# One sort key read into a register ahead of the first transfers instead of two, and all eight read at once after them

## The chip, the cores and the metric

The kernel runs on one core of a Trainium2 chip. The metric is the device time of one execution in microseconds (us); lower is better. In the profile the engines are called PE (TensorE, the matrix engine; PEld is its weight load), DVE (VectorE), ACT (ScalarE), POOL (GpSimd) and SP (SyncE, which here only issues transfers). A name with a q behind it (SPq, PEldq, POOLq) is an engine's own instruction queue: register loads, waits and DMA issues.

## The reference

```python
def _L0_cond_ref(x, cat_ids, W, b):
    selected_W = W[cat_ids]
    selected_b = b[cat_ids]
    return jnp.einsum('bti,bio->bto', x, selected_W) + selected_b[:, None, :]
x = x + _L0_cond_ref(x, itok_B_0_30, L0_cond_W, L0_cond_b)
```

x is [128, 128, 512] in float32: 128 batches of 128 rows. Each batch has a class, drawn from 0 to 30; W holds 32 matrices of 512x512 and b 32 rows of 512. Each batch is multiplied by its class's matrix, the class's bias row is added, and x itself is added.

## The kernel before, in words

The batches are worked in the order of their class, so that each class's weights are loaded once. In this data class 0 has six batches, class 1 three and class 2 nine, out of 128 batches in all. The residual is folded into the weights: GpSimd adds 1 to their diagonal (L236, L244, L260). float32 precision is reached with three products of rounded parts: xh and wh are the high parts of x and W, xl and wl the rests, and a batch is 12 matmuls (four slices of the contraction, three products), all at L436 except for the first batch. A chunk of 128 of the 512 contraction rows of a class's weights is called a chunk here; the weights of class 0 come as chunks 0 and 1 together (L284), chunk 2 (L285) and chunk 3 (L173), those of class 1 as two halves (L163).

The order of the batches is found on the chip. The ids arrive (L160), VectorE makes one sort key for each batch out of id and position (L328) and takes the eight largest (`top`, L330); the batch numbers of the first eight batches in sorted order follow from these keys. The full order, `tbc`, follows later (L343). SP needs a batch's number in a register before it can issue the load of its x, since the number is part of the address: `load(i)` takes it from `first[i]` (L168) for the first eight batches and from `tbc` afterwards (L150, eight at a time).

SP issues in the order of its program: x of batch 0, chunk 3 of class 0's weights, x of batch 1, first half of class 1's weights, then x of batches 2 and 3, bias row 0, the second half of class 1's weights, x of batch 4, the weights of class 2 (after a wait for the first batch's matmuls, L195 and L196), x of batch 5, bias row 1, and on with one x load and one store a batch.

```python
eng.wait_ge(s_t0, 1)
eng.load(first[:2], top[0:1, 0:2])
```

Each x goes through ACT (xh at L299, a copy into PSUM at L302) and DVE (xl at L348). The first batch is special: its first two slices are multiplied unsplit as soon as x has landed (L450), the other two in parts (L460), for which chunk 3 passes POOL (L236), ACT (L306) and DVE (L357). Class 1 is split by POOL in two halves (L244, L246, L248), every later class whole (L260, L268, L272). The bias rows of classes 2 and 3 are loaded by POOL behind the weights of class 3, which POOL issues once class 1 is split and bias row 1 has landed (L251). PE may begin class 2 only when these bias rows have landed (L277, then the semaphore `s_w`). Batches 6, 7 and 8 are of class 1; batch 9 is the first of class 2.

Of the kernel before, what the change touches and what calls it, by code (L numbers as in the profile page):

```python
# [5 lines left out]
def cond_resid(nc, xt, ids, W, bias, out):  # L6
# [31 lines left out]
    with ExitStack() as ctx:  # L38
        def sb(name, shape, dt):
            return ctx.enter_context(nc.sbuf_tensor(name, shape, dt))  # L40
# [25 lines left out]
        top = sb("top", [1, 8], i32)  # L66
# [57 lines left out]
        def raw(c, k0, k1):  # L124
            return wr[:, c % NR, k0 * D:k1 * D]
# [11 lines left out]
        def bias_load(eng, j0, j1, done):  # L137
            at = slice(j0 * D, j1 * D)
            eng.dma_start(bb[:, at].rearrange("p (c d) -> p c d", c=j1 - j0),  # L139
                          bias[j0:j1, :].rearrange("(a c) d -> a c d", a=1).to_broadcast([128, j1 - j0, D]))\  # L140
               .then_inc(done, 16)

        def table(eng, name, src, n, lo, hi, ahead=8):

            regs = [eng.alloc_register(f"{name}{i}") for i in range(ahead)]

            def get(i):
                if i % ahead == 0:
                    m = min(ahead, n - i)
                    eng.load(regs[:m], src[0:1, i:i + m])  # L150
                return eng.snap(regs[i % ahead], min_val=lo, max_val=hi)
            return get

        def x_load(eng, i, b):
            eng.dma_start(xs[:, i % NX, :, :], xt[b, :, :].rearrange("a p (k t) -> (a p) k t", k=KT))\  # L155
               .then_inc(s_x[i % NX], 16)

        @block.sync
        def _(eng):
            eng.dma_start(idr[:, :], ids.rearrange("(a n) -> a n", a=1)).then_inc(s_id, 16)  # L160
            def w1_load(h):
                k0, k1 = W1[h]
                eng.dma_start(raw(1, k0, k1), W[1, :, k0 * D:k1 * D]).then_inc(s_w1[h], 16)  # L163

            first = [eng.alloc_register(f"first{i}") for i in range(8)]

            def sorted_first(i):
                return (B - 1) - eng.snap(first[i], min_val=0, max_val=C * B - 1) % B  # L168

            eng.wait_ge(s_t0, 1)  # L170
            eng.load(first[:2], top[0:1, 0:2])  # L171
            x_load(eng, 0, bass.ds(sorted_first(0), 1))
            eng.dma_start(raw(0, 3, KT), W[0, :, 3 * D:]).then_inc(s_w0[2], 16)  # L173
            ahead = table(eng, "la", tbc, B, 0, B - 1)
            behind = table(eng, "st", tbc, B, 0, B - 1)

            def load(i):
                b = sorted_first(i) if i < 8 else ahead(i)
                if i == NX:
                    eng.wait_ge(s_xb, 2)  # L180
                    eng.wait_ge(s_mm, 2)
                elif i > NX:
                    eng.wait_ge(s_pt, i - NX)
                x_load(eng, i, bass.ds(b, 1))

            load(1)
            w1_load(0)
            eng.load(first[2:], top[0:1, 2:])
            load(2)
            load(3)  # L190
            bias_load(eng, 0, 1, s_b0[0])
            w1_load(1)
            load(4)
            eng.wait_ge(s_wd, KT)
            eng.wait_ge(s_raw, 1)  # L195
            eng.dma_start(wr[:, 0, :], W[2, :, :]).then_inc(s_w2, 16)  # L196
            load(5)
            bias_load(eng, 1, 2, s_b0[1])
            eng.wait_ge(s_tab, 1)
            for i in range(B):  # L200
                if i + AHEAD < B:
                    load(i + AHEAD)
                b = behind(i)
                eng.dma_start(out[bass.ds(b, 1), :, :].rearrange("a t d -> (a t) d"), os[:, i % NO, :])\
                   ._wait_ge(s_fin, i + 1).then_inc(s_o[i % NO], 16)
            for i in range(B - NO, B):
                eng.wait_ge(s_o[i % NO], 16 * (i // NO + 1))
# [285 lines left out]
```

## Time and profile before

| | before |
|---|---|
| median of 3 runs | 361.57 us (361.54 to 361.67) |
| the profiled execution | 361.55 us |
| its span, first to last instruction | 359.8 us |
| granted TensorE clock, mean | 0.999 |
| PE busy | 353.9 us (98%) |
| POOL busy | 268.6 us (75%) |
| DVE busy | 172.9 us (48%) |
| ACT busy | 146.6 us (41%) |
| mean DMA rate | 304 GB/s |

The profiled execution is 0.02 us below the median, and the span leaves out 1.75 us of it, which lie before the first and behind the last instruction. PE is busy almost all the time; the other engines have room on the whole, though not at each moment.

### The profile page before, as it was taken

To read this page: it belongs to the slowest core of one execution; us is meant where nothing else is said; L and a number is where in the kernel's file an instruction comes from. 1 tells how busy PE (TensorE), PEld (TensorE's weight loads), DVE (VectorE), ACT (ScalarE), POOL (GpSimd) and SP (SyncE) were. 2 spreads that over 40 slices of the span, in tenths; PEclk is the share of its full clock that TensorE was granted. 3 is DMA by queue.
4 is the path that set the end of the run, shared out by engine and by line. 5 is a ranking of instruction groups with operands and counts; after the bars stand their busy time and mean duration, and the time that the engine had idled before them with its cause. 6 is when DMAs were issued, how large, how long until landed. Compare 5 with 4: busy or idle time off the path is not lost.

```text
span 359.8 us, 6800 instructions
## 1 busy us (share of the span) xinstructions
PE 353.9 (98%) x1554; PEld 289.4 (80%) x1554; DVE 172.9 (48%) x278; ACT 146.6 (41%) x262; POOL 268.6 (75%) x148
## 2 busy tenths in 40 slices
PE   7999999999999999999999999999999999999996
PEld 2788888888888888888888888888888888888884
DVE  5754454535544454454454454445445445445442
ACT  4554353416443434343343344344344343434420
POOL 3797999998648698799964999799979899934000
PEclk9999999999999999999999999999999999999999
DMA  6999998999986999889996899989997999965532
GB/s 218 334 375 374 383 371 289 305 373 380 310 298 241 366 289 307 301 297 382 352 335 232 289 387 307 341 296 376 318 339 262 369 370 311 316 201 195 183 117 89
DMA packets 43381, 109.51 MB, mean 304 GB/s; under 512 B 4817, under 2 KB 4818, under 8 KB 38610
## 3 DMA queue, kind: packets, MB, share of 16 engines
q1 hardware_dynamic: 37730, 70.01, 54.1%
q0 software_dynamic: 5328, 38.28, 30.9%
q10 hardware_dynamic: 288, 0.79, 0.6%
q8 instruction: 18, 0.29, 0.3%
q14 instruction: 17, 0.14, 0.1%
HBM read 75.50 MB, written 33.55 MB: 303 GB/s over the span
## 4 chain that ended last, share of the span: by engine, by line
PE 96%; DMA 1%; DVE 0%; SPq 0%; issue 0%; ACT 0%; POOL 0%
PE pA L436 96%; DMA wr<-w 1%; DMA idr<-ids 0%; PE pA L460 0%; DVE os L383 0%; SPq L171 0%; ACT wh L306 0%; POOL wr L236 0%; SPq L155 0%; DVE top L330 0%; DVE key L328 0%; SPq L168 0%; PE pA L464 0%
## 5 line engine op out<-in xcount | busy, mean ns | idle before, releaser
L383 DVE TENSOR_TENSOR os<-pA,bb 128x512 f32<-128x512 f32 x128 | 88.5, 691 | 167.0 <-PE pA L436 166.8
L299 ACT ACTIVATE xh<-xs 128x512 fp32r<-128x512 f32 x127 | 80.3, 632 | 195.1 <-PE pA L436 115.7
L272 POOL TENSOR_TENSOR wl<-wr,wh 128x2048 fp32r<-128x2048 f32 x30 | 138.7, 4623 | 2.5
L436 PE MATMUL pA<-wh,xh 128*128 x508 | 135.9, 389 | 0.3 <-issue 0.3
L436 PE MATMUL pA<-wl,xh 128*128 x508 | 135.8, 389 | 0.0
L436 PE MATMUL pA<-wh,xl 128*128 x508 | 135.6, 389 | 0.0
L436 PEld LDWEIGHTS pA<-wh,xh 128*128 128x128 f32 x508 | 95.3, 188 | 20.0 <-issue 0.3
L436 PEld LDWEIGHTS pA<-wh,xl 128*128 128x128 f32 x508 | 95.3, 188 | 19.8
L436 PEld LDWEIGHTS pA<-wl,xh 128*128 128x128 f32 x508 | 95.3, 188 | 19.8
L348 DVE TENSOR_TENSOR xl<-pT,xh 128x512 fp32r<-128x512 f32 x127 | 86.7, 682 | 13.2 <-ACT pT L302 13.1
L268 POOL TENSOR_SCALAR wh<-wr 128x2048 fp32r<-128x2048 f32 x30 | 57.6, 1920 | 36.6 <-PE pA L436 34.8
L302 ACT ACTIVATE pT<-xs 128x512 f32<-128x512 f32 x127 | 74.0, 583 | 0.0
L260 POOL TENSOR_TENSOR wr<-wr,ident 128x512 f32<-128x512 f32 x30 | 39.2, 1305 | 0.7
L226 POOL DMA_DIRECT2D wr<-w x29 | 17.2, 592 | 11.1 <-POOL wl L272 8.0
L236 POOL TENSOR_TENSOR wr<-wr,ident 128x128 f32<-128x128 f32 x4 | 1.8, 472 | 4.5 <-DVE num L340 2.8
L390 PE MATMUL pA<-fill 128*128 128x512 bf16 (+2 forms) x14 | 4.0, 436 | 1.2 <-DVE fill L322 1.2
L248 POOL TENSOR_TENSOR wl<-wr,wh 128x1024 fp32r<-128x1024 f32 x2 | 4.8, 2404 | 0.2
L139 POOL DMA_DIRECT2D bb<-bias x8 | 4.3, 534 | 0.2 <-issue 0.2
L306 ACT ACTIVATE wh<-wr 128x512 fp32r<-128x512 f32 x4 | 2.4, 621 | 3.5 <-POOL wr L236 3.5
L357 DVE TENSOR_TENSOR wl<-wr,wh 128x512 fp32r<-128x512 f32 x4 | 2.7, 691 | 1.7 <-ACT wh L306 1.6
L244 POOL TENSOR_TENSOR wr<-wr,ident 128x256 f32<-128x256 f32 x2 | 1.5, 732 | 2.7 <-DVE wl L357 2.1
L390 PEld LDWEIGHTS pA<-fill 128*128 128x128 bf16 x14 | 1.3, 122 | 2.3 <-issue 2.1
(51 smaller groups left out, 20.1 us busy)
## 6 DMA issues: line engine op xcount, KB each, us to landing
xs<-xt SPq DMA_DIRECT2D x128, 256.0 KB, 5.7
out<-os SPq DMA_DIRECT2D x128, 256.0 KB, 5.1
wr<-w POOLq DMA_DIRECT2D x29, 1024.0 KB, 7.6
bb<-bias POOLq DMA_DIRECT2D x7, 1024.0 KB, 9.0
wr<-w SPq DMA_DIRECT2D x2, 512.0 KB, 5.8
wr<-w SPq DMA_DIRECT2D x1, 1024.0 KB, 8.1
wr<-w ACTq DMA_DIRECT2D x1, 512.0 KB, 3.7
bb<-bias SPq DMA_DIRECT2D x2, 256.0 KB, 6.7
```

The source lines that it names most:

```text
L139: eng.dma_start(bb[:, at].rearrange("p (c d) -> p c d", c=j1 - j0), bias[j0:j1, :].rearrange("(a c) d -> a c d", a=1).to_broadcast([128, j ...
L226: eng.dma_start(wr[:, c % NR, :], W[c, :, :]).then_inc(s_wr[c % NR], 16)
L248: eng.tensor_tensor(wl[:, at], half, wh[:, at].bitcast(f32), ALU.subtract).then_inc(s_wp, 1)
L260: eng.tensor_tensor(eye, eye, ones_on(KT), ALU.add).then_inc(s_ri, 1)
L268: eng.tensor_scalar(wh[:, at], wr[:, c % NR, :], 1.0, 1.0, ALU.mult, ALU.mult).then_inc(s_wh, 1)
L272: eng.tensor_tensor(wl[:, at], wr[:, c % NR, :], wh[:, at].bitcast(f32), ALU.subtract).then_inc(s_wp if c == 2 else s_w, 1)
L299: eng.activation(xh[:, i % NH, :, :], xs[:, i % NX, :, :], ACT.Copy).then_inc(s_xh, 1)
L302: eng.activation(pT[i % NT][:, :, :], xs[:, i % NX, :, :], ACT.Copy).then_inc(s_pt, 1)
L348: eng.tensor_tensor(xl[:, i % NH, :, :], pT[i % NT][:, :, :], xh[:, i % NH, :, :].bitcast(f32), ALU.subtract).then_inc(s_xl, 1)
L383: eng.tensor_tensor(os[:, i % NO, :], pA[i % NA][:, :], bb[:, bass.ds(at, D)], ALU.add)._wait_ge(s_mm, i + 2).then_inc(s_fin, 1)
L390: eng.matmul(pA[0][:, 0:w], fill[:, 0:128], fill[:, 0:w], start=True, stop=True)
L436: mm = eng.matmul(pA[i % NA][:, :], xp[:, i % NH, k, :], wp[:, bass.ds(at + k * D, D)], start=(n == 0), stop=(n == 3 * KT - 1))
```

## The change

SP loads one sort key ahead of batch 0's x and chunk 3, and all eight keys in one load right behind them. The load of the remaining six keys, which stood behind the first half of class 1's weights, is gone.

```diff
             eng.wait_ge(s_t0, 1)
-            eng.load(first[:2], top[0:1, 0:2])
+            eng.load(first[0], top[0:1, 0:1])
             x_load(eng, 0, bass.ds(sorted_first(0), 1))
             eng.dma_start(raw(0, 3, KT), W[0, :, 3 * D:]).then_inc(s_w0[2], 16)
+            eng.load(first, top[0:1, :])
             ahead = table(eng, "la", tbc, B, 0, B - 1)
             behind = table(eng, "st", tbc, B, 0, B - 1)
...
             load(1)
             w1_load(0)
-            eng.load(first[2:], top[0:1, 2:])
             load(2)
             load(3)
```

On SP, at the start of the program, the order changes as follows. TENSOR_LOAD is the load of keys into registers, the two ISA rows in front of a DMA are the arithmetic on its address, `xs<-xt` is an x load, and `wr<-w` a load of weights (128x512 is chunk 3, 128x1024 the first half of class 1).

```order
 L155 DMA xs<-xt 128x512
 L173 DMA wr<-w 128x512
+L174 TENSOR_LOAD top
 L168 ISA
 L155 ISA
 L155 DMA xs<-xt 128x512
 L163 DMA wr<-w 128x1024
-L188 TENSOR_LOAD top
 L168 ISA
 L155 ISA
```

The second load of keys has moved up past two transfers, batch 1's x and the first half of class 1's weights. The number of instructions on SP stays 562, and the orders of the other four engines are the same in both programs.

## Rows read from the trace of the kernel before

**Rows 1.** Waits of PE between 11 and 356 us: total us, times, longest.
```profile
PE pA L436 <- issue: 0.3, 1, 0.3
```

**Rows 2.** Chain that ended last, in order of time: start us, us, what.
```profile
2.66 0.66 SPq L171
...
3.72 0.39 SPq L155
...
4.16 3.81 DMA wr<-w
...
8.03 0.54 POOL wr L236
...
8.59 0.64 ACT wh L306
...
10.78 345.75 PE pA L436 x1524
```

**Rows 3.** Loads into registers by line: min/median/max ns, first and last start us.
```profile
L171 SPq TENSOR_LOAD <-top x1: 663/663/663, 2.7 to 2.7; - x1
...
L188 SPq TENSOR_LOAD <-top x1: 1281/1281/1281, 5.8 to 5.8; - x1
...
L405 PEldq TENSOR_LOAD <-top x1: 487/487/487, 3.2 to 3.2; - x1
...
L150 PEldq TENSOR_LOAD <-tbc x32: 328/332/747, 10.0 to 341.4; - x32
L150 SPq TENSOR_LOAD <-tbc x31: 520/532/1289, 13.1 to 336.5; - x31
```

**Rows 4.** Timeline of SP: start us, us, engine, line, operation.
```profile
4.97 0.34 SPq L155 DMA_DIRECT2D xs<-xt  x1
5.35 0.42 SPq L163 DMA_DIRECT2D wr<-w  x1
...
11.71 0.67 SPq L139 DMA_DIRECT2D bb<-bias  x1
```

**Rows 5.** Transfers issued at 3.72, 4.97, 5.35, 11.71, 21.45: KB, us to landing.
```profile
xs<-xt SPq DMA_DIRECT2D x1, 256.0 KB, 2.7
...
xs<-xt SPq DMA_DIRECT2D x1, 256.0 KB, 3.6
...
wr<-w SPq DMA_DIRECT2D x1, 512.0 KB, 5.1
...
bb<-bias SPq DMA_DIRECT2D x1, 256.0 KB, 8.3
...
bb<-bias POOLq DMA_DIRECT2D x1, 512.0 KB, 10.4
```

**Rows 6.** Busy time by stretch; the last two numbers are DMA share and GB/s.
```profile
6.00:7.00 1.00, 0.57 (x2) 0.34 (x3) 0.69 (x1) 1.00 (x4) 0.34 (x1) 1.00 0.61 172
```

**Rows 7.** Timeline of ACT, PE, POOL: start us, us, operation [idle before <-releaser].
```profile
9.13 0.61 ACT L299 ACTIVATE xh<-xs 128x512 fp32r<-128x512 f32 x1
...
9.27 0.50 PE L460 MATMUL pA<-wh,xh 128*128 128x512 f32 x1 [0.40 <-ACT wh L306]
...
10.63 0.74 POOL L244 TENSOR_TENSOR wr<-wr,ident 128x256 f32<-128x256 f32 x1 [2.07 <-DVE wl L357]
...
15.65 0.73 POOL L244 TENSOR_TENSOR wr<-wr,ident 128x256 f32<-128x256 f32 x1 [0.60 <-DMA wr<-w]
...
20.71 0.74 POOL L226 DMA_DIRECT2D wr<-w  x1 [0.70 <-DMA bb<-bias]
21.45 0.56 POOL L139 DMA_DIRECT2D bb<-bias  x1
```

**Rows 8.** PE's queue, released for batches 1 and 9, then batch 9's first weight load.
```profile
L436 PEldq FUSED_REGOPS  x1: 108/108/108, 10.6 to 10.6; - x1
...
L436 PEldq FUSED_REGOPS  x1: 91/91/91, 31.9 to 31.9; - x1
...
32.44 0.87 PEld L436 LDWEIGHTS pA<-wh,xl 128*128 128x128 f32 x4
```

## The prediction

> **What bounds the kernel now.** I read the waits of PE first. Between 11 and 356 us PE waits for others once, 0.3 us [rows 1]; the chain that ended last says the same, since from 10.78 us on it is 345.75 us of L436 without a break, then the last addition [rows 2]. So there are only two ways for an edit at the start to move the end: the moment at which the unbroken stretch begins, or a hole torn into it. Neither SP nor the transfers bound the middle.
>
> Before 10.78 us the chain is one path [rows 2]: SP reads its keys (2.66 us, 0.66 us long), issues x of batch 0 (3.72) and chunk 3 (4.16); chunk 3 takes 3.81 us to land; then POOL's diagonal (0.54), ACT's high part (0.64) and, from 9.27 on [rows 7], the last four matmuls of the first batch; then batch 1 begins. Chunk 3, not x, is the late one: x landed 2.7 us after its issue [rows 5], at 6.4, chunk 3 at 7.97.
>
> **The change part by part.**
>
> *The first load reads one key and not two.* Everything on the path from 2.66 on moves with it, one for one. The load of two keys took 0.663 us [rows 3]. One key on SP is nowhere in the trace. The nearest row is PE's load of one key from the same tile, half a microsecond later: 0.487. The loads of four registers on PE have a median of 0.332, so a load can be as short as 0.33 at least there; from above, nothing says that one key must be shorter than two. Bounds 0 and -0.33; I take -0.15, close to 0.663 - 0.487 = 0.18 and to the slope of the two loads of `top` on SP, (1.281 - 0.663) / 4 = 0.155 a key.
>
> *Eight keys are read behind chunk 3, and the six-key load is gone.* The new load stands ahead of x of batch 1 and of the first half of class 1. Its length: the SP loads of eight registers from `tbc` have 0.520 / 0.532 / 1.289 (minimum, median, maximum of 31), while six registers from `top`, also right behind two DMA issues, took 1.281 [rows 3]. So the number of registers doesn't set the length alone. The straight line through the loads of `top` gives 0.663 + 6 x 0.155 = 1.59. Bounds 0.52 and 1.59; I take 1.3, the row in the same place of the queue.
>
> The Trainium skill speaks to this in two places. DMA: Bandwidth & Descriptors, Latency and other measured facts, gives a load of this kind a floor of about 600 ns; the rows of 328 and 520 ns lie below it, so here the measurement decides. Runtime: NRT & Kernel Launch, Instruction fetch mechanics, prices such loads at some 200 ns a register; by that rule the first load would save 0.2 and the eight keys would take 1.6, an estimate, while the row of eight registers in 0.532 contradicts it and those of `top` agree roughly.
>
> With 1.3 the issue of batch 1's x goes from 4.97 to 4.97 - 0.15 + 1.3 + 0.04 (the step between two instructions) = 6.16, and class 1's first half from 5.35 to 6.54: both 1.2 us later (0.4 to 1.5 with the bounds). From x of batch 2 on, SP has one load less behind it: removed 1.28, added 1.3, minus 0.15, so about 0.1 earlier (bounds -0.9 and +0.3). Its queue is behind that the same until the wait at L195 for the first batch's matmuls, and bias row 1, issued at 11.71 [rows 4], moves with PE's start.
>
> *Who waits for batch 1's x.* It was issued at 4.97 and took 3.6 us [rows 5], so it landed at 8.6, but ACT came to it at 9.13, from chunk 3's high part, and was done at 9.74 [rows 7]. PE's queue was released for batch 1 at 10.6 [rows 8]. With PE 0.15 earlier, xh must be done by about 10.45, so the landing may be as late as 10.45 - 0.61 - 0.1 = 9.7. Issued at 6.16 it lands at 9.8 with the old 3.6, and at 8.9 with the 2.7 us that batch 0's x took on an otherwise emptier queue. Between 6 and 7 us the DMA engines were busy only 61% of the time at 172 GB/s [rows 6], so the queue isn't full there and the shorter time is the nearer one. Price: 0, with bounds 0 and (issue 6.5, landing 10.1) +0.4.
>
> *Who waits for class 1's first half.* It landed at 10.45 (5.35 + 5.1); POOL took it at 10.63, released by DVE. At 15.65 POOL began the second half, after a wait of 0.60 for its landing, so a half takes 15.05 - 10.63 = 4.4 us [rows 7]. So the first half may be up to 0.6 + 0.2 later for nothing. 1.2 later it costs POOL 0.4, if the transfer keeps its 5.1 us; 1.5 later, 0.7. It went behind batch 1's x in the same queue, and chunk 3 is out of its way now, so I expect 4.5 rather than 5.1, and no delay.
>
> *And class 2.* This is the narrow place behind the start. POOL split class 1 until 20.0 and bias row 1 landed at 11.71 + 8.3 = 20.0 too; then POOL issued at 20.71 and 21.45 the weights of class 3 and the bias rows 2 and 3, which landed 10.4 us later [rows 4, 5, 7], at 31.85. PE's queue went on at 31.9, and the first weight load of batch 9 was at 32.44 [rows 8]. From release to weight load takes about 0.17, as at batch 1 (10.78, the first matmul there, less 10.6); so the spare time there is 0.54 - 0.17 = 0.37 us. A PE that comes 0.15 earlier uses 0.15 of it. No hole, price 0. Later classes have not let PE wait before either [rows 1], and nothing of theirs changes but this shift.
>
> *Chunk 3's own transfer.* It took 3.8 us where x took 2.7, and batch 1's x was issued 0.8 us behind it. If that traffic slowed it, it now lands up to 1.1 earlier. PE could use 0.4 of that, the time for which it stood idle ahead of the matmuls on chunk 3 at 9.27 [rows 7]. The later transfer can hardly slow an earlier one in the same queue, so I take 0 and keep -0.4 as a bound.
>
> **Sum.** -0.15 (first load) + 0 (batch 1's x) + 0 (class 1, class 2) + 0 (chunk 3) = -0.15. Against the profiled execution's 361.55 that is 361.40, and against the median of 361.57 it is 361.42; I say 361.4.
>
> **The rivals.**
>
> *Nothing moves.* One key takes SP as long as two. For it: loads of one, four and eight registers differ less by number than by moment. 361.57.
>
> *Batch 1's x becomes late.* It keeps 3.6 us, the eight keys take 1.3 to 1.6, and PE begins batch 1 up to 0.4 later than it could: 361.4 + 0.1 to 0.4, 361.5 to 361.8. For it speaks that three transfers are in flight; against it the 61% of the DMA share.
>
> *The bias rows of class 2 come late: slower.* Class 1's first half lands 1.2 to 1.5 later, POOL is 0.4 to 0.7 late at 20.71, and the bias rows land that much later. Of this 0.37 is spare, so a hole of up to 0.35: 361.6 to 361.9. The landing of 10.4 us lies in a stretch with full DMA engines; if the new order there makes it 1.1 us later or more (0.37 + 0.72), the kernel ends above 362.3, measurably slower.
>
> *Chunk 3 lands early.* -0.15 - 0.4 = -0.55, and with a first load of 0.33 us -0.73: 361.0 to 360.8. For it speaks the 3.8 us beside the 2.7. But the spare 0.37 at batch 9 stands against it: PE would reach class 2 before its bias rows unless they come earlier too, and the gain ends at 361.2. Only with both is it measurably faster.
>
> **How the numbers follow.** A measurement of this kernel tells a change from none at about 0.2%, 0.72 us: above 362.3 or below 360.85. My forecast has 0.45; nothing moves 0.15; x of batch 1 late 0.13; bias rows late within 0.72 us 0.12, beyond it 0.07; chunk 3 early 0.08, of which 0.04 beyond 0.72. The range reaches from 360.95 (early chunk, not held at batch 9) to 362.1 (a hole of 0.5, bias rows 0.9 late) and leaves out about 0.12. The same cases give faster 0.04, same 0.89, slower 0.07.
>
> **What the profile after would show.** The load at L171 at about 0.5 us; x of batch 0 issued at 3.57 and chunk 3 at 4.0; a load at L174 of about 1.3 us; x of batch 1 issued near 6.2 and landed by 9.7; the unbroken stretch of L436 beginning at 10.6; POOL's second half still begun near 15.6; PE's queue released for batch 9 near 31.9 with no idle time of PE behind 11 us. The prediction is wrong if PE waits for ACT at batch 1, if POOL issues class 3 later than 21.1, or if chunk 3 takes less than 3 us.

## The result, and the profile after

The changed kernel has a median of 360.81 us over 22 executions against 361.68 us of the kernel before over 22, a ratio of 0.9979 with a 95% interval of 0.9972 to 0.9985: faster by about 0.2%, some 0.8 us. The forecast was 361.4, with a range from 360.95 to 362.1, so the result lies 0.14 us below the range.

The median hides how the times lie. Of the 22 executions 16 took 360.71 to 361.02 us, five 361.50 to 361.55, one 362.15. The kernel before never went below 361.51 in 22, and spread from there to 362.51. The profiled execution of the changed kernel is one of its later group: 361.55 us, span 359.8, the same as the profile of before. So the two profiles show what the change did to each step, and the reason why nothing came of it in that execution. The chain that ended last, start and us (to compare with [rows 2]):

```profile
2.67 0.47 SPq L171
...
3.53 0.39 SPq L155
...
3.97 3.81 DMA wr<-w
...
7.85 0.73 POOL wr L236
...
8.60 0.64 ACT wh L306
...
9.29 1.22 PE pA L460 x4
...
10.78 345.73 PE pA L436 x1524
```

The first load is 0.19 us shorter, x of batch 0 and chunk 3 are issued 0.19 earlier, and chunk 3 lands 0.19 earlier. Then GpSimd's fourth addition (L236) begins at 7.85 instead of 8.03 and ends at 8.57 or 8.58 as before: the whole gain is lost in this one operation, which takes 0.73 instead of 0.54 [rows 2]. Its timeline beside VectorE's:

```profile
7.56 0.69 DVE L357 TENSOR_TENSOR wl<-wr,wh 128x512 fp32r<-128x512 f32 x1
7.85 0.72 POOL L236 TENSOR_TENSOR wr<-wr,ident 128x128 f32<-128x128 f32 x1 [1.51 <-DMA wr<-w]
```

The addition begins inside VectorE's operation and ends 0.33 after its end at 8.25. The profile counts four of these additions, of which the median took 0.456 (min/median/max in ns):

```profile
L236 POOL TENSOR_TENSOR wr<-wr,ident x4: 455/456/721, 5.1 to 7.8; 128x128 f32<-128x128 f32 x4
```

The loads of keys, and SP's timeline behind them (against [rows 3, 4]):

```profile
L171 SPq TENSOR_LOAD <-top x1: 470/470/470, 2.7 to 2.7; - x1
...
L174 SPq TENSOR_LOAD <-top x1: 551/551/551, 4.4 to 4.4; - x1
```

```profile
5.35 0.34 SPq L155 DMA_DIRECT2D xs<-xt  x1
5.73 0.43 SPq L163 DMA_DIRECT2D wr<-w  x1
6.54 0.34 SPq L155 DMA_DIRECT2D xs<-xt  x1
```

Eight keys took 0.551 us, not 1.3. Batch 1's x is only 0.38 later than before, and batch 2's x, formerly issued at 7.45, is 0.91 earlier. That reaches far: bias row 1 took 7.5 us instead of 8.3, and the bias rows of classes 2 and 3, issued by POOL 0.02 later than before, landed after 9.2 us instead of 10.4 [rows 5]:

```profile
bb<-bias POOLq DMA_DIRECT2D x1, 512.0 KB, 9.2
```

### The profile page after: what moved, and what is told of

Its sections match the earlier page's. It is cut to its first block, busy times and chain, and to the rows that moved or that the text cites. A ratio compares the mean times of both kernels' runs of the same rounds, so it can differ in the third digit from the quotient of the medians.

```text
span 359.8 us, 6800 instructions
## 1 busy us (share of the span) xinstructions
PE 354.4 (99%) x1554; PEld 289.5 (80%) x1554; DVE 172.3 (48%) x278; ACT 146.6 (41%) x262; POOL 268.6 (75%) x148
## 4 chain that ended last, share of the span: by engine, by line
PE 96%; DMA 1%; DVE 0%; SPq 0%; issue 0%; POOL 0%; ACT 0%
PE pA L436 96%; DMA wr<-w 1%; DMA idr<-ids 0%; PE pA L460 0%; POOL wr L236 0%; DVE os L383 0%; ACT wh L306 0%; SPq L155 0%; SPq L171 0%; DVE top L330 0%; DVE key L328 0%; SPq L168 0%; PE pA L464 0%
## 5 line engine op out<-in xcount | busy, mean ns | idle before, releaser
L436 PE MATMUL pA<-wh,xh 128*128 x508 | 135.9, 389 | 0.3 <-issue 0.3
L436 PE MATMUL pA<-wl,xh 128*128 x508 | 135.8, 389 | 0.0
L436 PE MATMUL pA<-wh,xl 128*128 x508 | 135.6, 389 | 0.0
L436 PEld LDWEIGHTS pA<-wh,xh 128*128 128x128 f32 x508 | 95.3, 188 | 20.1 <-issue 0.3
L436 PEld LDWEIGHTS pA<-wh,xl 128*128 128x128 f32 x508 | 95.3, 188 | 19.8
L436 PEld LDWEIGHTS pA<-wl,xh 128*128 128x128 f32 x508 | 95.3, 188 | 19.8
L236 POOL TENSOR_TENSOR wr<-wr,ident 128x128 f32<-128x128 f32 x4 | 2.0, 522 | 4.3 <-DVE num L340 2.8
L357 DVE TENSOR_TENSOR wl<-wr,wh 128x512 fp32r<-128x512 f32 x4 | 2.7, 690 | 1.4 <-ACT wh L306 1.4
```

Of the source, the lines that this page charges most:

```text
L436: mm = eng.matmul(pA[i % NA][:, :], xp[:, i % NH, k, :], wp[:, bass.ds(at + k * D, D)], start=(n == 0), stop=(n == 3 * KT - 1))
```

## The experiments

In each of the five series the kernel before was timed on the same chip. Its medians were 361.94, 361.94, 361.80, 361.74 and 361.76 us; the lowest of all its 166 executions, those of the result included, is 361.51. An execution below 361.3 us is called early in what follows. Two executions far outside (513.98 us of before, 2053.52 us of one variant) are left out of what follows. "Half" is the first half of class 1's weights.

### First series: is the gain made at chunk 3?

**e1_after_again**: the changed kernel, not edited.

> The changed kernel once more, unchanged, for a profile of an execution near 360.75 us. Theory A (chunk 3 races against a VectorE operation): the times fall into two groups, near 360.75 and near 361.52. In the profile of after, GpSimd's fourth addition (L236) began at 7.85 us, inside VectorE's operation of 7.56 to 8.25, took 0.72 instead of 0.45 us and ended at 8.58, as in the kernel before. In an execution of the faster group chunk 3 should land before 7.3 us, the addition should take about 0.45 and end before 7.9, and L436 should begin near 10.0 instead of 10.78. Theory B (the gain is made at batch 9 or later): L436 begins near 10.78 in both groups, and the difference stands behind it.

Measured: 361.04 us median, 360.74 to 361.56, seven of 11 below 361.3; ratio 0.9977 (0.9968 to 0.9986). The profile fell into the later group again, but is worth more than one of the earlier would have been. Chunk 3 landed 0.27 us sooner than in the other profile, and nothing came of that either:

```profile
7.55 0.69 DVE L357 TENSOR_TENSOR wl<-wr,wh 128x512 fp32r<-128x512 f32 x1
7.58 0.99 POOL L236 TENSOR_TENSOR wr<-wr,ident 128x128 f32<-128x128 f32 x1 [1.24 <-DMA wr<-w]
```

The addition began 0.03 behind VectorE's operation and took 0.99 us, to end at 8.57 once more.

**e2_two_then_eight**: the second part of the change alone.

```diff
-            eng.load(first[0], top[0:1, 0:1])
+            eng.load(first[:2], top[0:1, 0:2])
```

> The changed kernel with two keys, not one, in the first load; eight keys behind chunk 3 as in after. It takes away the 0.19 us that the first load gave and keeps the later issue of batch 1's x. Theory A1 (chunk 3 is faster because batch 1's x and class 1's half come later behind it): a group near 360.8 to 360.95 us remains, median below 361.2. Theory A2 (the 0.19 us of the first load alone carry chunk 3 over the edge): all executions near 361.5, as before.

Measured: 361.54 us median, 360.83 to 362.47; five of 12 at 360.83 to 361.20; ratio 0.9986 (0.9976 to 0.9996). Chunk 3 is issued at 4.16 here as in before, and still there are executions that before never has. So A1 holds in part: what follows chunk 3 matters. With the shorter first load the share is larger (7 of 11 in the same series). Its profile is of the earlier group, 360.94 us. Chunk 3 took 3.3 us, and the addition just went ahead of VectorE's operation:

```profile
7.50 0.46 POOL L236 TENSOR_TENSOR wr<-wr,ident 128x128 f32<-128x128 f32 x1 [1.17 <-DMA wr<-w]
7.55 2.40 DVE L357 TENSOR_TENSOR wl<-wr,wh 128x512 fp32r<-128x512 f32 x3
```

0.08 us decides between this profile and the last: an addition begun at 7.50 ends at 7.96, one begun at 7.58 at 8.57. L436 began at 10.17 instead of 10.78, and there was no idle time of PE behind it.

**e3_vector_waits**: VectorE's second L357 waits until all four additions are done.

```diff
+            eng.wait_ge(s_ri, KT)
             for k in LOW[1:]:
                 low_w(k)
```

> The changed kernel, but VectorE starts its second L357 operation only when GpSimd's fourth addition is done. Theory A (while VectorE's operation on two SBUF inputs runs, GpSimd's addition stands still): the addition takes 0.45 us instead of 0.72 where chunk 3 lands near 7.8; ACT's fourth L306 begins near 8.3, L436 near 10.5, so the slower group moves from 361.52 to about 361.25; the faster group stays. Rival (the addition took 0.72 for a reason of its own, or waits for late bytes of chunk 3): the addition still ends at 8.58 and VectorE only comes later, 361.5 to 361.8.

Measured: 360.98 us median, 360.78 to 361.48; ratio 0.9975 (0.9966 to 0.9984). The times now fill the space: 360.78 to 360.98 (six), 361.13, 361.26, 361.45 to 361.48 (three). None stands at 361.5 to 361.56, where three of 11 of the changed kernel stood; the latest moved by less than 0.1 and not by the 0.25 that I expected. A tendency for theory A, within what 11 executions can tell. The profile, of 360.82 us, can't settle it: chunk 3 had landed at 7.2, so the addition stood ahead of the operation that was made to wait. It began inside VectorE's operation before that (7.04 to 7.47) and again ended 0.31 behind its end:

```profile
7.27 0.51 POOL L236 TENSOR_TENSOR wr<-wr,ident 128x128 f32<-128x128 f32 x1 [0.93 <-DMA wr<-w]
```

**e5_chunk3_first**: chunk 3 needs no key, and is issued ahead of the wait for them.

```diff
+            eng.dma_start(raw(0, 3, KT), W[0, :, 3 * D:]).then_inc(s_w0[2], 16)
             eng.wait_ge(s_t0, 1)
             eng.load(first[0], top[0:1, 0:1])
             x_load(eng, 0, bass.ds(sorted_first(0), 1))
-            eng.dma_start(raw(0, 3, KT), W[0, :, 3 * D:]).then_inc(s_w0[2], 16)
             eng.load(first, top[0:1, :])
```

> The changed kernel, but chunk 3, whose address needs no key, is issued by SP ahead of the wait for the keys, so it lands before batch 0's x. Theory A: GpSimd's fourth addition follows the third directly and ends before 7.2 us, every execution is in the faster group or below it, 360.5 to 360.8 us, unless the traffic makes chunk 2 or batch 0's x late. Theory B (batch 9 holds): no change to after, two groups.

Measured: 360.88 us median; ten of 12 at 360.57 to 361.05, two at 362.30 and 362.62; ratio 0.9973 (0.9960 to 0.9986). In its profile chunk 3 had landed at 5.48, GpSimd made all four additions in a row, and L436 began at 9.91, in an execution of 360.64. With chunk 3 out of the way nothing stands at 361.5: the plateau there belongs to chunk 3. The two at 362.3 and above are new and are taken up in the fourth series and in the last section.

### Second series: the pause behind chunk 3, and the later transfers

**e4_before_vector_waits**: e3's added wait, in the kernel before.

> The kernel before, but VectorE starts its second L357 operation only when GpSimd's fourth addition is done. In the kernel before chunk 3 landed at 7.96 us, the addition began at 8.03 and took 0.53, VectorE's operation ending at 8.24. Theory A (an addition that begins while VectorE's operation runs stands still until its end): without it the addition takes 0.45, so about 0.1 us is gained, best executions near 361.45, and executions near 361.0 may appear where chunk 3 lands at 7.6 and was held until now. Rival (nothing is held): the lowest time stays at 361.51 or rises.

Measured: 361.94 us median, 361.59 to 362.70; ratio 1.0004 (0.9995 to 1.0013). No gain in time. The profile shows why: chunk 3 came later still, at 8.09, so there was nothing to be held. The addition itself took 0.45, with VectorE's operation behind it:

```profile
8.16 0.45 POOL L236 TENSOR_TENSOR wr<-wr,ident 128x128 f32<-128x128 f32 x1 [1.82 <-DMA wr<-w]
...
8.65 0.63 ACT L306 ACTIVATE wh<-wr 128x512 fp32r<-128x512 f32 x1 [1.13 <-POOL wr L236]
8.65 0.69 DVE L357 TENSOR_TENSOR wl<-wr,wh 128x512 fp32r<-128x512 f32 x1 [1.19 <-POOL wr L236]
```

This settles nothing, either for the time or for the operation: begun at 8.16, the addition ended at 8.61, and the held ones end at 8.57, so a hold by VectorE until 8.25 could not have been seen in it.

**e7_more_quiet**: the kernel before, with the six keys in two loads of three behind chunk 3.

```diff
             eng.dma_start(raw(0, 3, KT), W[0, :, 3 * D:]).then_inc(s_w0[2], 16)
+            eng.load(first[2:5], top[0:1, 2:5])
+            eng.load(first[5:], top[0:1, 5:])
...
             w1_load(0)
-            eng.load(first[2:], top[0:1, 2:])
```

> The kernel before (two keys first), but its other six keys are read in two loads of three directly behind chunk 3, so batch 1's x and class 1's first half follow chunk 3 by about 1.7 us instead of 0.8. Theory A1 (traffic issued close behind chunk 3 slows it): chunk 3, issued at 4.16 as in before, lands before 7.4, most executions lie in 360.8 to 361.0, more of them than with 1.36 us between them (5 of 12). Rival A2 (only the earlier issue counts): 361.5 and above, as before. If batch 1's x becomes late instead, L436 waits for ACT's L299 and times lie at 361.2 or above in one group.

Measured: 361.39 us median, 360.95 to 362.46, six of 11 at 361.39 or below; ratio 0.9987 (0.9977 to 0.9997). Again executions below 361.5 with chunk 3 issued at 4.16 (five of the 11 are early), so what follows chunk 3 counts. But a longer pause is no better than e2's 0.54 us; in the profiled execution chunk 3 took 3.4 us, the addition began at 7.65 and was held for 0.91, 361.57 us in all.

**e8_half_behind**: the changed kernel with the half directly behind chunk 3.

```diff
             eng.dma_start(raw(0, 3, KT), W[0, :, 3 * D:]).then_inc(s_w0[2], 16)
+            w1_load(0)
             eng.load(first, top[0:1, :])
...
             load(1)
-            w1_load(0)
```

> The changed kernel, but the first half of class 1's weights, which needs no key, is issued directly behind chunk 3, ahead of the load of eight keys. The first load's gain of 0.19 us stays, the pause behind chunk 3 is gone. Theory A1 (traffic issued close behind chunk 3 slows it): chunk 3 lands at 7.7 or later, no executions below 361.3, median 361.5 or more. Rival A2 (the pause does not matter): two groups as in after, with more than half near 360.75.

Measured: 363.32 us median, 362.22 to 364.83, ratio 1.0047 (1.0030 to 1.0063): the only variant that is clearly slower. Chunk 3 took 3.9 us. The loss itself is the other one of my rivals, at last seen: batch 1's x, issued at 5.89 behind 512 KB, landed at 10.9, and PE waited for ACT. The chain and PE's wait in that profile:

```profile
5.89 5.03 DMA xs<-xt
10.94 0.63 ACT xh L299
```

```profile
PE pA L436 <- ACT xh L299: 1.3, 1, 1.3
```

In the changed kernel batch 1's x was issued 0.38 us later than in before and still landed at 8.4; here, issued 0.92 later, it landed 2.3 later, and that is too late.

**e10_old_load_back**: the changed kernel; behind chunk 3 only the second key, the other six where they stood before.

```diff
-            eng.load(first, top[0:1, :])
+            eng.load(first[1], top[0:1, 1:2])
...
             w1_load(0)
+            eng.load(first[2:], top[0:1, 2:])
```

> The changed kernel, but behind chunk 3 only the second key is read, and the other six where they stood before, behind class 1's first half. The start up to there is as in after within 0.1 us; x of batches 2 to 4, bias row 0 and class 1's second half are issued later by the length of that load, 0.5 to 1.3 us. Theory C (the second part of the gain is that the later transfers and with them the bias rows of classes 2 and 3 land earlier, so that PE does not stand at batch 9): the groups near 360.75 and 361.52 stay, but executions 0.3 to 1.0 us above them appear again, as in before. Rival: the spread of before comes from the start alone, and the times are those of after.

Measured: 361.77 us median, 361.54 to 362.86; ratio 0.9999 (0.9990 to 1.0008). The early issue of chunk 3 was kept (4.00), and no execution came below 361.54: the early issue of chunk 3 alone gives nothing that 11 executions show (the interval is 0.1%, 0.36 us, either way). What it lacks is the space behind chunk 3: the single key was read in 0.29 us, and the half came 1.51 us behind chunk 3 instead of 1.76. The profile is of an execution of 362.13 and shows a second way to lose, the chain running through the bias rows:

```profile
12.06 8.95 DMA bb<-bias
...
21.69 0.74 POOL wr L227
...
22.43 10.45 DMA bb<-bias
...
33.10 324.00 PE pA L437 x1428
```

```profile
PE pA L437 <- POOLq L278: 0.3, 1, 0.3
```

Bias row 1 landed 1 us later than in before, POOL issued class 3 a us later, and PE stood at batch 9. The row prints 0.3 us of idle time behind the modelled end of the matmul before; from start to start the pause is 0.66 us where matmuls otherwise come 0.23 apart, 0.43 more. This is the mechanism of my slower rival, in a variant.

### Third series: each half of the gain alone

**e11_before_chunk3_first**: e5's move in the kernel before, with its loads of two and six keys.

> The kernel before with chunk 3 issued ahead of the wait for the keys, its loads of two and six keys left as they are. The first batch is then as early as in the changed kernel's faster group, but the later transfers are held by the load of six keys behind class 1's half (1.28 us). Theory C (the bias rows of classes 2 and 3 decide at batch 9): PE begins L436 near 10.0 and then stands at batch 9 for 0.3 to 1.2 us; few or no executions below 361.2, median 361.3 to 361.9. Rival (the start alone decides): as the changed kernel with chunk 3 first, median 360.9.

Measured: five executions at 360.59 to 360.70, six at 362.36 to 362.59; median 362.36 without the outlier and 362.43 with it; ratio 0.9993 (0.9978 to 1.0008). The five refute theory C as I had put it: with the old loads left in place and PE 0.8 us earlier, the bias rows held nothing up. So the margin at batch 9 is not what gives or denies the gain in general. The six at 362.36 and above are the group of e5 again.

**e12_six_before_half**: the kernel before, with the load of six keys ahead of the half.

```diff
             load(1)
-            w1_load(0)
             eng.load(first[2:], top[0:1, 2:])
+            w1_load(0)
```

> The kernel before, but its load of six keys stands ahead of class 1's first half and behind batch 1's x. The first load of two keys and the traffic right behind chunk 3 stay. From the loads measured so far (0.29 to 0.68 us behind an x or chunk 3, 1.28 behind class 1's half three times) it should take 0.5 to 0.7 us, so batch 2's x and what follows come 0.6 to 0.8 us earlier. Theory C: the start stays in the slower group, 361.5, with hardly an execution below it, but those above 361.7, some half of the kernel before, go: median 361.56, highest below 362. Rival: the spread stays as in before.

Measured: 361.91 us median, 361.58 to 362.52, ratio 1.0005 (0.9997 to 1.0014): no change. The premise failed: the load took 1.283 us in this place too, so nothing behind it came earlier. It says nothing on theory C; on the load it says that its length does not come from the issue ahead of it. It does bear on what slows chunk 3: the half came 2.50 us behind chunk 3 here, and batch 1's x 0.81 behind it as in before, and none of the 11 executions was early. So keeping the half away is not enough to give the early group.

**e13_chunk3_first_one_load**: chunk 3 ahead of the keys, then one load of all eight.

> A candidate for the best: chunk 3 ahead of the wait for the keys, then all eight keys in one load, then the x of batches 0 and 1. Eight keys cost batch 0's x about 0.06 us against one key and batch 1's x comes 0.5 us earlier. If the rows so far hold, median 360.6 to 360.9, lowest near 360.6; batch 0's x late (shared traffic) would show as L450 beginning after 6.7.

Measured: 360.97 us median; seven of 12 at 360.63 to 361.03, five at 361.94 to 362.80; ratio 0.9992 (0.9977 to 1.0007). No better than e5.

**e14_after_third**: the changed kernel once more.

> The changed kernel for the third time, beside the others on the same chip: two groups as before, lowest near 360.74, median between 360.75 and 361.1. In an execution of the faster group GpSimd's fourth addition begins before VectorE's operation at 7.55, takes 0.45 us, and L436 begins near 10.0.

Measured: 361.53 us median, and only one of 11 below 361.3, at 360.89; ratio 0.9991 (0.9982 to 1.0000). The expected median was missed: how often chunk 3 wins the race differs from series to series (16 of 22, 7 of 11, 1 of 11). The profile fell on the one early execution and shows the changed kernel at its best, as theory A had it:

```profile
7.46 0.46 POOL L236 TENSOR_TENSOR wr<-wr,ident 128x128 f32<-128x128 f32 x1 [1.11 <-DMA wr<-w]
7.56 0.90 DVE L357 TENSOR_TENSOR wl<-wr,wh 128x512 fp32r<-128x512 f32 x1
```

Here the addition was first, and it is VectorE's operation that is held: 0.90 us instead of 0.69. L436 began at 10.13.

### Fourth and fifth series: the spread of before, and a better version

**e17_before_again**, **e18_before_once_more**: the kernel before, for profiles.

> The kernel before, unchanged, for a profile of one of its executions above 361.7. Theory C: PE stands at batch 9 for the bias rows of classes 2 and 3, as it did for 0.43 us in the execution of 362.13 with the old load put back. Theory D: the first batch runs at half pace and L450 x4 takes more than 2.2 us. Neither shows if this execution is at 361.55.

> As the one before it, a second try for a profile of the kernel before above 361.7: theory C a hole of PE near 32.4 us, theory D a slow first batch.

Measured: 361.79 and 361.77 us, and neither theory: no hole near 32.4, no slow first batch. Chunk 3 simply came after VectorE's operation. In e18 the chain reads:

```profile
4.16 4.06 DMA wr<-w
...
8.28 0.47 POOL wr L236
...
10.96 345.78 PE pA L436 x1524
```

Landed at 8.2, the addition takes its 0.46 and ends later than 8.58; L436 begins 0.18 later than at 361.55, and in e17 (landed at 8.28) 0.24 later. The time follows, 361.79 less 361.55 being 0.24. Executions of before above 362.1 remain without a profile.

**e16_chunk3_first_again** is e5's kernel, **e15_chunk3_first_fill** adds two fill matmuls to it, of no use to the result:

```diff
-            warm(1)
+            warm(3)
             warm(1, 256)
```

> The changed kernel with chunk 3 ahead of the wait for the keys, and two more fill matmuls of 512 columns (of no use to the result) ahead of the first batch. In that order of transfers some executions lie at 362.3 to 362.8 because the first batch's matmuls run at about half their pace (L450 x4 took 3.78 instead of 1.98 us in one of 362.56). Theory D (the idle time of PE ahead of batch 0's x, 0.8 us, or too little work in front of it decides that): the slow group goes, all executions at 360.6 to 361.1. Rival (it is decided earlier, or by something else): about a third of the executions stay at 362.3 or above.

> The changed kernel with chunk 3 ahead of the wait for the keys, once more, beside the one with more fill matmuls: lowest near 360.57; a sixth to a half of the executions at 362.3 or above, the others at 361.1 or below.

Measured: e15 360.85 us median, all nine at 360.63 to 361.07, ratio 0.9974 (0.9964 to 0.9984); e16 360.91, two of nine at 362.37 and 362.43, ratio 0.9980 (0.9969 to 0.9991). The profile of e16 is of 362.37. The first batch's matmuls there, then those of e15 (min/median/max in ns):

```profile
L450 PE MATMUL pA<-wr,xs x4: 934/1061/1220, 6.7 to 9.4; 128*128 128x512 f32 x4
```

```profile
L450 PE MATMUL pA<-wr,xs x4: 592/592/697, 6.7 to 8.1; 128*128 128x512 f32 x4
```

**e19_first_fill_again** and **e20_after_fourth**: e15's kernel and the changed kernel, on one chip.

> The version with chunk 3 ahead of the wait for the keys and two more fill matmuls, once more, beside the changed kernel on one chip: all executions at 360.6 to 361.1, median near 360.85, none at 362.3.

> The changed kernel beside it: executions near 360.75 and near 361.52 in shares that have differed from chip to chip (16 of 22 below 361.3, 7 of 11, 1 of 11); median between 360.8 and 361.53, so at or above that of the version with chunk 3 first.

Measured: e19 360.90 us median, 360.64 to 361.24 in 12, ratio 0.9967 (0.9953 to 0.9982); e20 361.35, six of 12 at 361.17 or below and six at 361.53 to 361.72, ratio 0.9982 (0.9971 to 0.9993). Chunk 3 first with more fill is the better version, 0.45 us below the changed kernel in the median on this chip, and all its 21 executions in two series are below 361.3. The intervals against the kernel before overlap, so the size of its lead is less sure than its evenness.

## Why the prediction was wrong

**The mechanism.** Twelve profiles line up on one operation. VectorE's second L357 begins at 7.55 or 7.56 in each and, where it isn't held itself, runs to 8.25: it stands behind ACT's high part of chunk 2, which follows ACT's high part of batch 0's x at 6.60. That x had landed by 6.56 in all twelve, so a shift of SP did not move it (with chunk 3 first, where x landed at 6.6 to 6.8, it began at 7.60 to 7.79). What becomes of the fourth addition depends on when chunk 3 lands:

| kernel | batch 1's x behind chunk 3, us | half behind chunk 3, us | chunk 3 took | addition began, took | L436 began | us |
|---|---|---|---|---|---|---|
| e8 | 1.93 | 0.47 | 3.9 | 7.96, 0.60 | x late | 363.10 |
| before | 0.81 | 1.19 | 3.8 | 8.03, 0.53 | 10.78 | 361.55 |
| e18, before | 0.80 | 1.19 | 4.1 | 8.28, 0.46 | 10.96 | 361.77 |
| e17, before | 0.88 | 1.27 | 4.1 | 8.34, 0.46 | 11.02 | 361.79 |
| e10 | 1.12 | 1.51 | 3.8 | 7.86, 0.71 | 10.78 | 362.13 |
| after | 1.38 | 1.76 | 3.8 | 7.85, 0.72 | 10.78 | 361.55 |
| e1, after | 1.36 | 1.75 | 3.5 | 7.58, 0.99 | 10.78 | 361.55 |
| e14, after | 1.38 | 1.77 | 3.4 | 7.46, 0.46 | 10.13 | 360.89 |
| e20, after | 1.36 | 1.75 | 3.2 | 7.19, 0.58 | 10.00 | 361.04 |
| e2 | 1.37 | 1.75 | 3.3 | 7.50, 0.46 | 10.17 | 360.94 |
| e12 | 0.81 | 2.50 | 3.5 | 7.72, 0.84 | 10.78 | 361.77 |
| e7 | 2.30 | 2.68 | 3.4 | 7.65, 0.91 | 10.77 | 361.57 |

Seven additions that began between 7.58 and 8.03 all ended at 8.56 to 8.58, and L436 began at 10.77 or 10.78 wherever batch 1's x was there. Before 7.55 the addition is free, and L436 comes 0.6 to 0.8 earlier; one that begins behind 8.12 (an estimate: 8.57 less the 0.455 of an addition alone) ends later, and L436 comes later one for one, as in e17 and e18. (e20's 0.58 began inside VectorE's operation ahead, which ran from 7.04 to 7.46; it lost 0.24 us in two small holes near 12.6 and 13.0, hence 361.04, and e12 lost 0.17 in the same place, at batch 2.) The kernel before sat on or behind the late end of that plateau; the change moved chunk 3 by 0.19 through its issue, and, as it seems, by some tenths more through the pause behind it, so that about half of the executions come out at the early end: 30 of 56 in the result and three later series lie below 361.3, and none of 166 of before. That the landing of chunk 3 decides between the groups is shown by the profiles and by e5 and e11. That it lands sooner where less is issued close behind it is less sure. It rests on the shares of early executions (5 of 12 in e2 and 5 of 11 in e7, none in e10, e12 and before) and on the three columns of the table behind the name, one execution each, in which the changed kernel itself has 3.2 to 3.8 us with the same pause. Whether batch 1's x or the half does the slowing is not separated: in e8 only the half stood close, and chunk 3 took 3.9 us; in e12 only x did, chunk 3 took 3.5, and no execution was early.

The Trainium skill has this rule in SBUF — State Buffer, "SBUF: two separate sides": VectorE and GpSimd share a pair of ports as an exclusive lock, taken for a whole instruction by whichever starts first, also where a VectorE operation has two SBUF inputs and GpSimd's reads SBUF. This is just such a pair (wr and wh against wr and ident), and the traces agree: 0.99 us for an addition that came 0.03 late, 0.90 for the VectorE operation that came behind one (e14). Not all of an operation is held, though: the held additions end 0.31 to 0.33 behind VectorE's end, where one alone takes 0.455. By that rule every landing between 7.5 and 7.97 ends the addition at one and the same time, and 0.19 us gain nothing; the prediction did not use it.

**Point by point.** That PE is unbroken from 10.78 on, so that only its start and holes count, was right. The first load, priced at -0.15, measured -0.19. The failure lies in "Everything on the path from 2.66 on moves with it, one for one": between chunk 3's landing and ACT's work stood an operation whose end was set by VectorE. With the old pattern of loads behind chunk 3 it was worth nothing that could be seen (e10).

The second failure, and the one that made the forecast miss its range, is the step on *chunk 3's own transfer*: "The later transfer can hardly slow an earlier one in the same queue, so I take 0 and keep -0.4 as a bound." It took 3.2 to 3.8 us in the changed kernel and 3.8 to 4.1 in the kernel before, so the rival *Chunk 3 lands early*, given 0.08, was what happened in the larger part of the 22 executions. Its price was too small as well: I let PE use 0.4, the idle time printed ahead of 9.27, and L436 came 0.61 to 0.78 earlier. That idle time is counted from the printed end of the matmul before, and the next one can begin before that end, as e2 shows:

```profile
8.51 0.40 PE L460 MATMUL pA<-wh,xl 128*128 128x512 f32 x1
...
8.75 0.42 PE L460 MATMUL pA<-wh,xh 128*128 128x512 f32 x1
```

So PE came to chunk 3 at 8.75 and not 9.27, 0.52 earlier, and the matmuls without a pause took 0.08 less, though x of batch 0 and the matmuls on chunk 2 came no earlier in e2 than in before. In e20 they came 0.12 earlier on top. And the cap that I put on this rival did not exist. I let the spare 0.37 us at batch 9 end the gain at 361.2; no profile of an early execution has PE waiting there. The bias rows landed at 30.7 to 31.0 in e2, e14 and e20 and not at 31.9. That the old loads alone would not have held PE there is what e11 shows, with five executions below 360.8.

The term that was mis-sized by most is the second load: eight keys were priced at 1.3 us, "the row in the same place of the queue", with bounds from 0.52; they measured 0.55. So batch 1's x was issued at 5.35 and not 6.16, the half at 5.73 and not 6.54, and from batch 2's x on SP ran 0.91 earlier and not 0.1. (The bounds given there, 0.4 to 1.5 us, vary this load alone; with those of the first load they are 0.2 to 1.6, and 0.38 was measured.) That batch 1's x would cost nothing was right (issued at 5.35, landed at 8.4, taken by ACT at 9.14), and so was class 1: POOL began the half at 11.30 instead of 10.63 and the second one at 15.67 instead of 15.65, within its slack. The slower rival by way of the bias rows is real as a mechanism (e10, at batch 9), but the change moved away from it. None of the three signs of being wrong that I had named showed: PE did not wait for ACT at batch 1, POOL issued class 3 at 20.72, and chunk 3 took at least 3.2 us. The rows that did tell were the length of the load at L174 and the start of L436, forecast at 10.6 and found at 10.78 or at 10.0 to 10.2, but in no profile of the changed kernel between them.

## What to carry to other kernels

Follow a gain through every operation on its path and ask of each what else sets its end; where two engines exclude each other, a small shift is worth nothing or several times itself, depending on which side of an edge it falls. Look at single times and not only at the median: groups of them name the edge, and a profile tells only of the group it fell into. A transfer that needs nothing should be issued ahead of the wait and not behind it, but watch what it does to the transfer that it overtakes.

## What the runs showed of the hardware

**Loads of keys are priced by their count, except for eight.** SP's loads of `top` without a wait took 288 ns for one key (e10), 677 and 684 for three (e7), 1280 to 1285 for six (in seven profiles), but 536 to 551 for eight:

```profile
L174 SPq TENSOR_LOAD <-top x1: 288/288/288, 4.5 to 4.5; - x1
...
L189 SPq TENSOR_LOAD <-top x1: 1282/1282/1282, 6.0 to 6.0; - x1
```

```profile
L174 SPq TENSOR_LOAD <-top x1: 677/677/677, 4.7 to 4.7; - x1
L175 SPq TENSOR_LOAD <-top x1: 684/684/684, 5.4 to 5.4; - x1
```

That is 0.20 us a key with 0.09 on top. The loads of eight registers from `tbc` have a median of 0.532 in after too, with the longest at 1.39. A load behind the wait for the keys took some 0.18 more: 0.47 for one, 0.66 for two, 0.72 for eight (e13). The Trainium skill's Runtime: NRT & Kernel Launch, Instruction fetch mechanics, has 200 ns a register "even for bulk", for loads that it describes as coming from HBM, while these come from SBUF; the runs agree up to six and contradict it at eight. Whether it is the number eight or the alignment of its address that makes the difference was not tried.

**A first batch at nearly half pace.** In two profiles with chunk 3 first (e11 and e16) the first batch's matmuls came 0.85 us apart instead of 0.43 and L436 began at 11.83 and 11.63, 1.9 and 1.7 us later than in e5. The row of that stretch of e16 prints a granted clock of 1.00 all the same (the last three numbers are PEclk, DMA share and GB/s):

```profile
6.70:8.50 1.80, 1.78 (x2) 0.84 (x3) 1.75 (x4) 1.46 (x3) 0.71 (x1) 1.00 0.90 270
```

But the column prints 1.00 also where the trace has no entry of the clock. The first entry lies at 10.12 us in e16 and at 10.55 in e11, and between 4.13 and 7.31 in the other 18 profiles. The pace of the matmuls changes about there: in e16 those of L450 come 0.85 apart up to 9.4, and those of L460 from 10.44 on 0.23 apart as in e5, and in e1, whose first entry is at 4.66, fill matmuls of 512 columns come 0.43 apart at 4.02 and 0.23 apart at 5.33. So TensorE did the first batch of e11 and e16 at the lower of its two levels, 1.2 and not 2.4 GHz, which accounts for the length of the two profiled executions (362.56 and 362.37 us against 360.64). What makes the clock rise late in some of them stays open.

Just before its first batch PE had stood idle 0.4 us in e16 for batch 0's x, and its last two fill matmuls took 0.82 us together where e1 had 0.50; but e14 had 0.82 as well, with the first entry at 6.50, and then a first batch at nearly full pace. With two more fill matmuls none of 21 executions was later than 361.3; without them it was 9 of 33 in e5, e13 and e16 together, and 6 of 11 in e11. On one chip side by side it was none of nine (e15) against two of nine (e16), which is too few to tell them apart; that the fill prevents the slow first batch is likely and not shown.
